# Attention rows of maxima: SyncE instead of ScalarE sends them in four of eight slots

## The reference

```python
h = layernorm(x) * (1 + ca) + sa
qkv = einsum('btc,fc->btf', h, W_attn)          # 16 heads of 32
att = where(causal, einsum('bhqd,bhkd->bhqk', q, k), -inf)
out = einsum('bhqk,bhkd->bhqd', softmax(att / sqrt(32)), v)
x = x + ga * einsum('btc,oc->bto', out, W_proj)
h = layernorm(x) * (1 + cb) + sb
x = x + gb * (relu(relu(h W1 + b1) W2 + b2) W3 + b3)
```

## Time and profile before

| what | us |
|---|---|
| time, median of 3 runs (lowest to highest) | 1503.06 (1500.37 to 1503.61) |
| the profiled execution's own time | 1500.26 |
| its span, first to last instruction | 1498.5 |
| TensorE busy | 1432.5 (96%) |
| VectorE busy | 1111.7 (74%) |
| ScalarE busy | 811.2 (54%) |
| GpSimd busy | 447.9 (30%) |

### The profile page before, as it was taken

One profiled execution on the slowest core, in us unless ns is written; L12 is line 12 of the kernel. 1 busy time (PEld: TensorE's weight loads), 2 busy tenths in 40 slices (PEclk: granted clock), 3 DMA queues, 4 the chain that ended last, 5 costly groups with the idle time before them and its releaser, 6 DMA issues. The chain is left out here.

```text
span 1498.5 us, 30337 instructions
## 1 busy us (share of the span) xinstructions
PE 1432.5 (96%) x12048; PEld 1284.9 (86%) x12048; DVE 1111.7 (74%) x1955; ACT 811.2 (54%) x1468; POOL 447.9 (30%) x450
## 2 busy tenths in 40 slices
PE   7999999999999999988699999999999999999998
PEld 4578787887878878876599999999999999999998
DVE  4687777777877777668676666797766676788887
ACT  3366666667676767666555555566333333354331
POOL 2375765666576667655200000000000000000000
PEclk9999999999999999999799999999999999999999
DMA  8625354443534343473344444644756556589985
GB/s 275 157 55 128 93 135 94 110 114 78 125 88 122 83 122 82 101 203 116 106 148 148 148 149 148 221 173 150 271 199 218 204 211 235 210 290 311 298 298 181
DMA packets 126589, 247.15 MB, mean 165 GB/s; under 512 B 13672, under 2 KB 36200, under 8 KB 126448
## 3 DMA queue, kind: packets, MB, share of 16 engines
q1 hardware_dynamic: 122416, 241.56, 51.6%
q10 hardware_dynamic: 4032, 3.66, 0.8%
HBM read 114.58 MB, written 79.72 MB: 130 GB/s over the span
## 5 line engine op out<-in xcount | busy, mean ns | idle before, releaser
L537 POOL TENSOR_TENSOR prob_lo<-prob,prob_hi 128x512 f16<-128x512 f32 x256 | 300.6, 1178 | 162.1 <-ACT prob L670 161.7
L663 ACT ACTIVATE prob_hi<-key_score 128x512 f16<-128x512 f32 x320 | 191.1, 597 | 150.8 <-PE key_score L1000 149.3
L2399 PE MATMUL sum_b<-op,w 128*128 128x256 f32 x1728 | 217.9, 284 | 3.4 <-DVE p_c L1957 1.7
L887 PE MATMUL lin<-h_parts,wqkv 128*128 128x512 f32 x768 | 215.1, 403 | 3.7 <-POOL h_parts L497 2.8
L2399 PEld LDWEIGHTS sum_b<-op,w 128*128 128x128 f32 x1728 | 211.3, 192 | 5.7 <-issue 3.7
L845 DVE TENSOR_REDUCE row_max<-score 128x1 f32<-128x512 f32 (+2 forms) x384 | 180.3, 498 | 22.1 <-PE score L987 21.3
L670 ACT ACTIVATE prob<-key_score 128x512 f32<-128x512 f32 x320 | 190.6, 596 | 0.0
L887 PEld LDWEIGHTS lin<-h_parts,wqkv 128*128 128x128 f32 x768 | 139.4, 191 | 33.5 <-DVE h_parts L718 5.4
L987 PE MATMUL score<-stack 96*128 96x512 f32 (+3 forms) x512 | 154.7, 363 | 0.0
L2399 PE MATMUL sum_e<-op,w 128*128 128x256 f32 x1152 | 146.7, 284 | 2.3 <-issue 1.4
L1000 PE MATMUL key_score<-stack 98*128 98x512 f32 (+3 forms) x512 | 143.8, 343 | 4.7 <-DMA stack<-max_rows 4.7
(11 more groups left out here) (164 smaller groups left out, 2555.7 us busy)
## 6 DMA issues: line engine op xcount, KB each, us to landing
stack<-qk_parts SPq DMA_DIRECT2D x384, 128.0 KB, 2.4
late_op_whole<-y_dram SPq DMA_DIRECT2D x40, 512.0 KB, 5.3
y_dram<-u_c SPq DMA_DIRECT2D x32, 512.0 KB, 3.4
blk<-y_dram SPq DMA_DIRECT2D x32, 512.0 KB, 4.2
y_dram<-y_sum SPq DMA_DIRECT2D x24, 512.0 KB, 3.5
x_tiles<-x SPq DMA_DIRECT2D x32, 256.0 KB, 3.7
attn_dram<-o_rows SPq DMA_DIRECT2D x32, 256.0 KB, 2.3
attn_tiles<-attn_dram SPq DMA_DIRECT2D x8, 1024.0 KB, 6.1
```

What stands on the lines that cost most here:

```text
L537: nc.gpsimd.tensor_tensor(prob_lo[:, key[1] % 2, u, :], prob[:, u, :], prob_hi[:, key[1] % 2, u, :], ALU.subtract).then_inc(lo_pool, 1)
L663: nc.scalar.activation(prob_hi[:, q % 2, u, :], bank[:], ACT.Exp, scale=SOFTMAX_SCALE, bias=P_SHIFT)
L887: mm = nc.tensor.matmul(lin_bank_of((QK, f))[:], wqkv[:, wl, c, at:at + P], h[:, hl, c, :], start=(c == 0 and k == 0), stop=(c == NC_ - 1 ...
L2399: mm = nc.tensor.matmul(dst, w[:, wl, c, cols], data[:, dl, c, :], start=begin, stop=end, skip_group_check=again)
```

## The change

In slots 0, 1, 4 and 5 of a batch (in the first batch only 4 and 5) the two DMAs are issued by SyncE, at u = 2 behind whatever it has before. In the last batch slots 5 to 8 were SyncE's already; slots 0, 1 and 4 join them. The test `not first` goes, since the new condition is false where there is nothing to send. ScalarE leaves the pair out wherever `rows_on_sync` is true.

```diff
+SYNC_FREE = (0, 1, 4, 5)
...
     def rows_on_sync(b, p):
 
-        return b == B - 1 and NEXT_FROM < p <= PAIRS
+        if b == B - 1 and p > NEXT_FROM:
+            return p <= PAIRS
+        return p in SYNC_FREE and (b > 0 or p >= NEXT_FROM)
...
-                    if u == 2 and not first and rows_on_sync(b, p):
+                    if u == 2 and rows_on_sync(b, p):
                         n, q = behind(b, p, 1, first)
                         sp.wait_ge(turn_taken, 1 + PAIRS * n + q + 1)
                         for part in range(2):
```

## The result

| | before | after |
|---|---|---|
| median of the runs, us (6 each) | 1502.62 | 1518.68 |
| lowest to highest | 1500.37 to 1504.77 | 1514.44 to 1522.75 |
| the profiled execution, us | 1500.26 | 1518.73 |
| its span, us | 1498.5 | 1516.9 |
| mean granted TensorE clock | 0.988 | 0.982 |

The ratio is 1.0096, with a 95% interval of 1.0079 to 1.0114: the kernel is slower, by 16 us in the medians and 18 between the two profiled executions. The forecast was 1511.4, in a range of 1503 to 1522.

What follows compares the result with a forecast made beforehand. TensorE, busy 1432.5 of 1498.5 us, was taken to bound the kernel. The terms summed to +8.3 us on the profiled 1500.26, giving 1508.6, and 1511.4 for a median, with 8 in 10 between 1503 and 1522.

Steps and rivals of the forecast that it cites:

- New waits in slot 0: Batches 1 to 6: SyncE's rows, behind stack issues and x loads, reach TensorE late; +14.1 us.
- The latency of 3.2 us: Assumed time for a pair sent on SyncE to reach TensorE, taken between bounds of 3.1 and 4.8 us.
- Old gaps absorbed: Slots 0 and 1, batches 1 to 6: TensorE gaps after the stalled matmul go, 6.5 us in all, counted as -6.0.
- The clock in these waits: Slot-0 stalls, batches 1 to 6: TensorE's clock falls in two of six, about 2.5 us each; +5.0 us.
- none to three: Likeliest case: the forecast with none to three clock falls in the slot-0 stalls, 1506 to 1517 us; chance 0.50.
- all or most: Rival: the clock falls in all or most slot-0 stalls; +18 us, 1521, if in every one; chance 0.15.
- Batch 7, slot 4: Rows sent ahead of 1 MB loads end the 3.54 us wait, -3.3 us, and its clock fall, -2.5 us.
- The late thing next: Batch 7, slot 4: 1 MB loads go about 1.8 us later; without slack, 2 of the 3.3 us come back.
- Slot 5: Seven batches: rows stand behind the output store, margin 3.0 us against 3.2; 0.2 us each, +1.4 us.
- batch 7's slot 0: No x loads; rows come behind the stack issues, margin 2.3 us against 3.2; +0.9 us.
- batch 0: Slot 4 of batch 0: rows come behind the stack load of group 3, margin 1.6 us against 3.2; +1.6 us.
- Slot 4: Batches 1 to 6: without the issues ScalarE's modulation starts 0.5 us earlier, shortening TensorE's 1.72 us gap; -2.9 us.

Runs made afterwards that it cites:

- e1: Kernel before, with only the pair of slot 0 in batches 1 to 6 moved to SyncE; 1528.48 us, ratio 1.0156 to before.
- e4: The change, but in slot 0 of batches 1 to 6 SyncE issues the pair ahead of the four x loads; 1504.13 us, ratio 1.0000 to before.
- e5: Kernel before, but ScalarE sends slot 0's pair one unit later (u = 3) in batches 1 to 6; 1512.06 us, ratio 1.0066 to before.
- e6: The change plus ten extra matmuls on TensorE in slot 1, u = 0 of batches 1 to 6; 1510.48 us, ratio 1.0055 to before.
- e3: Kernel before, with only the pair of slot 4 in batch 7 moved to SyncE; 1503.78 us, ratio 0.9994 to before.
- e7: The change without slot 0 and batch 0, batch 7's x and gate loads issued behind slot 5's pair; 1491.94 us, ratio 0.9928 to before.
- e8: Kernel before, with only the pair of slot 4 in batches 1 to 6 moved to SyncE; 1496.55 us, ratio 0.9956 to before.

## Why the prediction was right in sign and low in size

- **New waits in slot 0: +14.1 forecast, +16.6 measured.** Place, cause and order were right (e1, e4). The latency of 3.2 us was too low beside x: 3.4 to 5.0. I had reasoned that most of the drain passes under the pair's own issue; e5 shows 3.2 to 5.2 us on the other queue as well.
- **Old gaps absorbed: -6.0 forecast, -5.2 measured** (6.5 before, 1.3 left in slots 0 and 1).
- **The clock in these waits: +5.0 forecast, +9.0 measured.** The number of falls was wrong: I took two, from one gap of 2.6 that had left the clock alone, and gave "none to three" a chance of 0.50 and "all or most" 0.15; there were five, one behind 1.6 us. With 2.5 us a fall I was high, at 1.2 to 2.3 measured. e6 shows the term directly. The Trainium skill ("TensorE: Matmul & The Clock Gate", section "HAM oscillation") tells of a kernel in which waits for a DMA of some 3 to 5 us throttled the clock each time round. Batch 5's wait of 4.4 us agrees; three of the five waits that cost the clock here were shorter than those, 1.6 to 3.0 us, so the runs go beyond what the section tells. The gap of 2.6 before 97 is shorter too, and was no evidence against it.
- **Batch 7, slot 4: -3.3 and -2.5 forecast, -0.4 measured.** This step failed, and by the most. "The late thing next" was asked for the loads behind the pair and not for the next pair: with TensorE 4.3 us ahead, slot 5's rows fell into the loads that slot 4's had escaped, a 6.2 us wait, and the clock fell there instead. e3 shows no gain from this pair, e7 that the loads ahead of slot 5's pair are the reason.
- **Slot 5: +1.4 forecast, 0 measured; batch 7's slot 0: +0.9, 0.1; batch 0: +1.6, +0.9.** My lower bound for the bare latency, 3.1 us, was no bound: the pair of batch 7's slot 0 was used 2.6 us after its first issue (640.31 to 642.93) with no gap on TensorE, and that of batch 0's slot 4, behind twelve stack loads, 2.6 us after its own (98.63 to 101.26) with a wait of 0.79. I had put a median over 128 KB transfers in place of the smallest time of a 4 KB one.
- **Slot 4: -2.9 forecast, -3.6 measured in the profile**, and more in the medians (e8).

The terms as measured: 16.6 - 5.2 + 9.0 - 0.4 + 0.1 + 0.9 - 3.6 = 17.4 us, the growth of the attention. Against the forecast of +8.3, batch 7 is off by 5.4, the clock by 4.0, the waits by 2.5 and the old gaps by 0.8, and the three small terms of slot 5, batch 7's slot 0 and batch 0 and the gain of slot 4 give back 3.6. So the result lies in the stated range through the width of the range; the sum had only about half of the loss. Of the signs that I had named, the slot-1 waits, the absorbed gaps and the slot-4 gap came; a clock of 1.00 in batch 7, falls in a third of the batches and a gap in slot 5 did not.

What I drew from the Trainium skill ("DMA: Bandwidth & Descriptors", section "Queues, rings and completion order"), from its statement that SyncE and ScalarE own separate rings between which the DMA engines take turns, was that ScalarE's rows would overtake queued loads. That does not show here: e5's pair took as long.

## What to carry to other kernels

Before a small transfer is moved to another engine's queue, lay that queue's issues and the moment of need side by side for each place: four places in a batch looked free of stack loads, and the one whose margin was 0.8 us on average lost, by itself, more than four times what all other pairs gained (+24 against -5). Where a wait of TensorE is removed, follow the next transfer of the same kind at its new, earlier time. And price a TensorE wait with the clock that it can cost, which here added 9.0 us to 16.6 us of waits.

## What the hardware showed that I had not expected

- The clock fell behind gaps as short as 1.6 us (1.72 in e3) and held behind two of 2.6 (and batch 1 of e5); the same gap in the same place sometimes cost it and sometimes not. It goes with the spread between the runs of one kernel: of the 28 runs of the kernel before beside e1 to e4, the ten with a mean granted clock of 0.986 or more have a median of 1501.9 us, the thirteen with 0.984 or less one of 1506.3. Where in those runs the clock fell is not known, since only one run of each kernel has a trace.
- A pair of 4 KB transfers behind 1 MB of x loads took 3.2 to 5.2 us from its first issue until TensorE could use it, on either queue (5.7 in batch 5 of e6), 2.6 with no load of x ahead, and 8.7 with three 1 MB loads ahead. Batches of the same code differed by 1.7 us in this; why was not found.
